# Attention and a routed expert layer on one core: each routed row written to a place of its own, instead of added into running sums

## The chip, the core and the metric

The kernel runs on one core of a Trainium2 chip. The metric is the device time of one execution in microseconds. The five engines (PE multiplies matrices, DVE and ACT work on rows of 128 partitions, POOL issues indirect DMAs and small operations, SP issues DMAs) each run their own list of instructions in order and wait for one another by semaphores; 16 DMA engines move the data.

## The reference, cut to what matters

```
x   = x + attention(layernorm(x), context)         # 32 batches x 100 tokens, width 256; context 361 x 192
h   = layernorm(x)
shared = gelu(h @ ws1 + bs1) @ ws2 + bs2
aff = softmax(h @ Wr + br)                         # 31 experts
routed = sum over the 3 experts e with the largest aff:
             aff[e] * (gelu(h @ We1[e] + Be1[e]) @ We2[e] + Be2[e])
out = x + shared + routed + h
```

There are 3200 tokens, so 9600 routed rows of 256 numbers (1 KB in float32), three for each token.

## The kernel before

**Stages.** The 3200 tokens are 25 tiles of 128. In the attention stage (a loop over steps i = -2 to 36, one batch of 100 tokens each, all engines staggered by a few steps) a tile's residual `resid = x + attention` is made by DVE (L754), normalized to `h` (L855), routed, and three indirect DMAs of POOL (L557) write its rows of `h`, with the experts, the weights and the token's number beside them, into lists per expert in DRAM (`xs`, printed as `expert_rows_in`). SP also stores `resid` (L395) and `h` (L396) of each tile to two DRAM arrays `sums[0]` and `sums[1]`, and once fills a third with zeros (L374).

**The middle.** When all tokens are routed, a table of at most 105 routed tiles (expert, first row) is worked out on DVE (L935 to L968) and PE. Beside it PE runs the shared layer for tiles 0 to 7; DVE copies its result into `tok` (L864).

**The routed loop.** For each of 105 tiles SP loads 128 rows of a list (L455, 6 buffers); PE transposes them (L1260), multiplies by the expert's first matrix (L1271) and the second (L1282, with the matrix in place); ACT copies the transposed rows (L715) and applies gelu (L689). DVE, in `tile`, takes out the token number (L993), finds the weight (L994, L996, L1000), copies the expert's first matrix for the tile after next into one of two buffers (L976, `fetch_w1`), and scales the product (L984, the row `y_sb`). POOL then adds the 128 rows into `sums[t % 3]` by an indirect DMA that accumulates (L579); it waits for the accumulation of three tiles before, since two into the same array at once could lose an addition.

**The closing.** After the last accumulation SP loads the three arrays, in 11 groups of 1 to 3 tiles (L473 to L475), DVE adds them (L1018, L1021) and adds the shared result: from `tok` for tiles 0 to 7 (L1025), and for the 17 late tiles from PSUM, where PE makes it meanwhile (L1177, L1186, L1187; DVE L1031). SP stores the groups to the output (L478). Groups of early and late tiles alternate: (8,11), (0,1), (11,14), (1,3) and so on to (7,8), (23,25).

The order of the work is written out by hand: each engine's list is the order of the calls below.

## Time and profile before

| | us |
|---|---|
| median of 3 runs | 494.28 |
| lowest and highest | 491.18, 496.79 |
| the profiled execution's own time | 494.56 |
| its span, first to last instruction | 492.90 |

The profile is of one execution. "Busy" is time in which an engine executes; `PEld` is PE's loading of weights, which overlaps its products. SPq, POOLq and ACTq are the engines' instruction queues, where a DMA's issue is seen. The granted clock is 1.00 at 2.4 GHz and 0.50 at 1.2 GHz. The stages lie at 0 to 216 us (attention), 216 to 233 us (table and shared layer), 233 to 446 us (routed loop) and 446 to 492.9 us (closing).

### The profile page before, as it was taken

The numbers are of one execution on the slowest core, as the hardware profiler recorded it, in microseconds if no ns is written. First come the engines' busy times: TensorE is split into PE (matmuls) and PEld (weight loads), VectorE is DVE, ScalarE is ACT, GpSimd is POOL, SyncE is SP. The second block draws the span as 40 slices with busy tenths as digits, with TensorE's granted clock in tenths as the row PEclk, the third lists the DMA queues.
The fourth block names the chain that finished last, engine by engine and source line by source line (L and its number), as shares of the span: only waits on it lengthen the run. The fifth ranks groups of instructions, "written<-read, shape, count | busy, mean of one in ns | idle before, by whom it ended". The sixth has DMA issues, their size and how long they took to land.

```text
span 492.9 us, 13620 instructions
## 1 busy us (share of the span) xinstructions
PE 461.0 (94%) x3168; PEld 400.0 (81%) x3168; DVE 357.1 (72%) x1614; ACT 253.7 (51%) x848; POOL 308.7 (63%) x316
## 2 busy tenths in 40 slices
PE   8899979999999998879999999999999999999991
PEld 8677757777777877668999898899999999999891
DVE  4958879999999997773567666666666666661784
ACT  1455747676767667462445454445554555543220
POOL 3312385858585857671588888788888888884000
PEclk9999999999999999989999999999999999999997
DMA  7555668877578944893599999898888888875999
GB/s 241 150 172 151 219 208 255 274 239 257 189 235 286 334 149 154 276 360 105 116 184 187 185 183 181 157 145 138 136 137 137 139 135 138 136 107 101 350 348 322
DMA packets 81151, 97.54 MB, mean 198 GB/s; under 512 B 9201, under 2 KB 65906, under 8 KB 81074
## 3 DMA queue, kind: packets, MB, share of 16 engines
q1 hardware_dynamic: 60786, 70.79, 46.9%
q0 software_dynamic: 19248, 25.40, 30.8%
q10 hardware_dynamic: 1040, 0.48, 0.5%
q8 instruction: 29, 0.48, 0.4%
q14 instruction: 48, 0.39, 0.3%
HBM read 54.91 MB, written 41.73 MB: 196 GB/s over the span
## 4 chain that ended last, share of the span: by engine, by line
PE 50%; DVE 15%; issue 10%; DMA 10%; SPq 5%; POOL 3%; ACT 2%; POOLq 0%; DVEq 0%; ACTq 0%
PE bank L1271 12%; PE bank L1282 12%; DMA sum<-y_sb,token 6%; PE bank L1260 3%; PE bank L1106 2%; PE bank L1107 2%; PE bank L1118 2%; DVE w_all L792 2%; PE bank L1158 2%; DMA xt<-expert_rows_in 2%; POOL sum L579 2%; DVE c L741 2%; DMA w_all<-sum 2%; PE bank L1186 2%; PE bank L1159 2%
## 5 line engine op out<-in xcount | busy, mean ns | idle before, releaser
L579 POOL DMA_INDIRECT sum<-y_sb,token x105 | 170.8, 1626 | 48.0 <-issue 24.1
L689 ACT ACTIVATE up<-bank,b_all 128x128 f32<-128x128 f32 x260 | 81.4, 364 | 102.2 <-PE bank L1271 66.1
L1271 PE MATMUL bank<-xtt,w1b 128*128 128x128 f32 x840 | 111.4, 276 | 0.3 <-ACT xtt L715 0.3
L1282 PE MATMUL bank<-w_all,up 128*128 x420 | 108.8, 382 | 0.1
L1271 PEld LDWEIGHTS bank<-xtt,w1b 128*128 128x128 f32 x840 | 102.1, 192 | 0.8 <-ACT xtt L715 0.5
L984 DVE TENSOR_SCALAR y_sb<-bank,gate,inverse 128x256 f32<-128x256 f32 x105 | 57.1, 544 | 55.4 <-PE bank L1282 54.7
L557 POOL DMA_INDIRECT expert_rows_in<-xt,slot x75 | 74.4, 992 | 24.6 <-issue 24.0
L1282 PEld LDWEIGHTS bank<-w_all,up 128*128 128x128 f32 x420 | 71.7, 191 | 6.1 <-issue 0.2
L976 DVE COPY w1b<-w_all 128x512 f32 x105 | 47.7, 454 | 18.1 <-PE bank L1271 7.5
L715 ACT ACTIVATE xtt<-bank 128x256 f32<-128x256 f32 x105 | 40.2, 384 | 39.3 <-PE bank L1260 38.7
L534 POOL TENSOR_TENSOR rs<-mv,eps_cols 128x5 f32<-128x5 f32 (+1 forms) x32 | 8.0, 252 | 62.2 <-DVE mv L849 62.0
L1260 PE MATMUL bank<-ident,xt 128*128 128x128 f32 x210 | 40.0, 273 | 0.7 <-DMA xt<-expert_rows_in 0.7
L1260 PEld LDWEIGHTS bank<-ident,xt 128*128 128x128 f32 x210 | 29.2, 141 | 11.9 <-DMA xt<-expert_rows_in 1.7
L536 POOL TENSOR_TENSOR rs<-rs,mhalf 128x5 f32<-128x5 f32 (+1 forms) x32 | 36.4, 1137 | 2.5
L1118 PEld LDWEIGHTS bank<-w_all 128*128 128x128 f32 (+1 forms) x192 | 24.1, 191 | 13.1 <-ACT w_all L630 12.5
L792 DVE TENSOR_SCALAR w_all<-w_all,mv,rs 128x192 f32<-128x192 f32 x96 | 31.1, 380 | 2.8 <-POOL rs L536 2.7
L1186 PE MATMUL bank<-w_all,up 128*128 128x256 f32 x100 | 27.3, 397 | 2.0 <-issue 0.8
L1118 PE MATMUL bank<-w_all 128*128 128x100 f32 (+1 forms) x192 | 27.8, 281 | 0.8 <-ACT w_all L630 0.8
L741 DVE BATCH_NORM_STATS2 c<-w_all 128x6 f32<-128x192 f32 x96 | 27.9, 345 | 0.2 <-DMA w_all<-in_ctx 0.2
L1177 PEld LDWEIGHTS bank<-tok,w_all 128*128 128x128 f32 x200 | 26.9, 199 | 1.2
L1177 PE MATMUL bank<-tok,w_all 128*128 128x128 f32 x200 | 27.5, 284 | 0.0
L1106 PE MATMUL bank<-w_all,tok 128*100 128x361 f32 x64 | 25.4, 478 | 0.0
(199 smaller groups left out, 883.4 us busy)
## 6 DMA issues: line engine op xcount, KB each, us to landing
xt<-expert_rows_in SPq DMA_DIRECT2D x105, 132.0 KB, 2.6
w_all<-in_w SPq DMA_DIRECT2D x47, 256.0 KB
w_all<-in_ctx SPq DMA_DIRECT2D x32, 288.0 KB, 3.1
w_all<-sum SPq DMA_DIRECT2D x15, 384.0 KB, 7.3
sum<-pad_rows SPq DMA_DIRECT2D x1, 3328.0 KB, 12.0
w_all<-in_x SPq DMA_DIRECT2D x25, 128.0 KB, 3.1
sum<-y_sb SPq DMA_DIRECT2D x25, 128.0 KB
sum<-xt SPq DMA_DIRECT2D x25, 128.0 KB
```

What stands on the lines that cost most here:

```text
L557: pool.indirect_dma_start(xs, bass.IndirectOffsetOnAxis(ap=slot[s4][:, k:k + 1], axis=0), h_sb[s4][:, :], None).then_inc(scattered[s4], 16)
L579: pool.indirect_dma_start(sums[s], bass.IndirectOffsetOnAxis(ap=token[sx][:, 0:1], axis=0), y_sb[sx][:, :], None, compute_op=ALU.add).then ...
L689: ins = act.activation(up[s][:, m * P:m * P + P], up_ps[s][:, m * P:m * P + P], ACT.Gelu, bias=b1_all[:, e, m:m + 1].rearrange("p o n -> p ...
L715: act.activation(xtt[s][:, :], tile_ps[s], ACT.Copy).then_inc(tile_t_copied, 1)
L792: ins = dve.tensor_scalar(z[s4][:, k, 0:D2], c_sb[s4][:, k, :], mv[s][:, k, 0:1], rs[s][:, 1, k:k + 1], ALU.subtract, ALU.mult)
L976: dve.tensor_copy(w1b[n.slot(2)][:, :], w1_all[:, bass.ds(e, 1), :].rearrange("p o n -> p (o n)"))\
L984: dve.tensor_scalar(y_sb[sx][:, :], down_ps[s], gate[s][:, 0:1], inverse[s][:, 0:1], ALU.mult, ALU.mult).then_inc(y_made, 1)
L1118: mm = pe.matmul(mix_ps, z[s4][0:KT[k], k, 0:P], probs_t[s][0:KT[k], k, :], start=(k == 0), stop=(k == 2))
L1177: mm = pe.matmul(up_ps[s][:, m * P:m * P + P], w1_all[:, NE, c * INTER + m * P:c * INTER + m * P + P], tok[:, c, cut(t)], start=(c == 0), ...
L1260: mm = pe.transpose(tile_ps[s][:, c * P:c * P + P], xt[sx][:, c * P:c * P + P], ident[:, :])
L1271: mm = pe.matmul(up_ps[s][:, m * P:m * P + P], w[:, c * INTER + m * P:c * INTER + m * P + P], xtt[s][:, c * P:c * P + P], start=(c == 0), ...
L1282: mm = pe.matmul(down_ps[s], up[s][:, m * P:m * P + P], w, start=(m == 0), stop=(m == 1))
```

## The change

- Every routed row goes to its own place in one DRAM array `routed_rows`, at row 768 + 3 * token + rank (rank 0, 1 or 2 of its expert for the token). The list rows carry three such places (`DST`) instead of the token's number; the padding rows carry none, and their rows go to one of the 768 spare rows. POOL's indirect DMA is a plain write, and waits for no earlier one; a buffer's earlier write is waited for by DVE, six tiles later.
- DVE's `tile` picks weight and place in one pass (2 x 3 numbers), reduces them before it copies the matrix, and makes the row numbers (`token`) after it.
- `x` is loaded into `base`, one place per tile in SBUF, and `resid` overwrites it there. ACT then turns it into resid + h in place, as base * (1 + rstd) - mean * rstd (`scale_base`): 8 tiles in the attention steps 22 to 29 and 17 in every second tile of the routed loop. For this all steps' mean and rstd are kept (`stats`), in the space of the two matrix buffers. SP's stores of `resid` and `h`, the fill with zeros and the waits for them are gone.
- DVE adds the shared result of tiles 0 to 7 onto `base` at once.
- The closing loads 11 times (3 KB in a row for each token: its three routed rows) instead of 33 times, and DVE adds the three onto `base`, then for late tiles the shared result.
- To make room, one more expert's first matrix is loaded early (24 instead of 23), the late loads are cut differently, and some small arrays move.

```diff
-WHO, EXPS, SUM, TOKEN = D1, D1 + TOP, D1 + 2 * TOP, D1 + 2 * TOP + 1
-ROW = TOKEN + 1
+WHO, EXPS, DST, SUM = D1, D1 + TOP, D1 + 2 * TOP, D1 + 3 * TOP
+ROW = SUM + 1
 SLOTS = 4
+XS = 6
+SPARE = XS * P
...
-    sums = [nc.dram_tensor(f"sum{k}", [TOKENS + P, D1], F32, kind="Internal").ap() for k in range(3)]
+    routed_rows = nc.dram_tensor("routed_rows", [SPARE + TOP * TOKENS, D1], F32, kind="Internal").ap()
...
+        base = sb("base", [P, TILES, D1])
+        shift = sb("shift", [P, 2, 39])
...
-        x_sb = [lend(1, P, D1) for _ in range(8)]
...
+        x_sb = [base[:, t, :] for t in range(TILES)]
...
+        w1b_all = sb("w1b_all", [P, 2, 2 * INTER])
+        fold_q = lend(1, P, 2 * (RQ + NE)).rearrange("p (c n) -> p c n", c=2)
+        first = w1b_all.rearrange("p s n -> p (s n)")
+        stats = first[:, 0:39 * 20].rearrange("p (i k n) -> p i k n", k=5, n=4)
...
+        FIRST_ROWS = 20
+        rows1 = w1_all[:, 0:30, :].rearrange("p e n -> p (e n)").rearrange("p (t k n) -> p t k n", k=TOP, n=D1)
+        rows2 = w2_all[:, 0:9, :].rearrange("p e n -> p (e n)")[:, 0:6 * TOP * D1].rearrange("p (t k n) -> p t k n", k=TOP, n=D1)
...
-                    sp.dma_start(sums[2].rearrange("(k p) n -> p k n", p=P),
-                                 pad_rows[:, 0:D1].unsqueeze(1).to_broadcast([P, TILES + 1, D1])).then_inc(spare_ready, 16)
-                    for k in range(2):
-                        sp.dma_start(sums[k][TOKENS:TOKENS + P, :], pad_rows[:, 0:D1]).then_inc(spare_ready, 16)
...
-                t = ends(i - 5)
-                if t is not None:
-                    sp.wait_ge(h_made, t + 1)
-                    alone(sp)
-                    sp.dma_start(sums[0][cut(t), :], resid[t % SLOTS][:, :]).then_inc(base_out[t % SLOTS], 16)
-                    sp.dma_start(sums[1][cut(t), :], h_sb[t % SLOTS][:, 0:D1]).then_inc(h_out[t % SLOTS], 16)
...
-            sp.wait_ge(resid_made, TILES)
+            sp.wait_ge(gates_made, TILES)
             alone(sp)
-            late1(23, 24)
+            late1(24, 26)
...
-            for s in range(3):
-                sp.wait_ge(added[s], len(range(s, NT, 3)) * 16)
-            def rows_of(dram, lo, hi):
-                return dram[lo * P:hi * P, :].rearrange("(k p) n -> p k n", p=P)
+            for s in range(XS):
+                sp.wait_ge(put[s], len(range(s, NT, XS)) * 16)
             for g, (lo, hi) in enumerate(GROUPS):
-                sp.dma_start(part0[:, lo:hi, :], rows_of(sums[0], lo, hi)).then_inc(rows_in[g], 16)
-                sp.dma_start(part1[:, lo:hi, :], rows_of(sums[1], lo, hi)).then_inc(rows_in[g], 16)
-                sp.dma_start(part2[:, lo:hi, :], rows_of(sums[2], lo, hi)).then_inc(third_in[g], 16)
+                rows = routed_rows[SPARE + TOP * lo * P:SPARE + TOP * hi * P, :]
+                sp.dma_start(rows_at(lo, hi).rearrange("p t k n -> p t (k n)"),
+                             rows.rearrange("(t p k) n -> p t (k n)", p=P, k=TOP)).then_inc(rows_in[g], 16)
             for g, (lo, hi) in enumerate(GROUPS):
-                sp.wait_ge(final_made, final_at[hi - 1])
-                sp.dma_start(rows_of(flat_out, lo, hi), part0[:, lo:hi, :]).then_inc(final_out, 16)
+                if lo < S_E:
+                    sp.wait_ge(sum_made, TOP * g + TOP)
+                else:
+                    sp.wait_ge(shared_added, late_tiles.index(hi - 1) + 1)
+                alone(sp)
+                sp.dma_start(flat_out[lo * P:hi * P, :].rearrange("(t p) n -> p t n", p=P), base[:, lo:hi, :]).then_inc(final_out, 16)
...
+                if i == SHIFT_STEP:
+                    pool.tensor_scalar(shift[:, 0, 0:18], stats[:, 0:18, 4, 3], 1.0, None, ALU.add).then_inc(first_shifts, 1)
+                    pool.tensor_tensor(shift[:, 1, 0:18], stats[:, 0:18, 4, 0], stats[:, 0:18, 4, 3], ALU.mult).then_inc(first_shifts, 1)
+                    pool.wait_ge(first_shifts, 2)
+                    pool.tensor_scalar(shift[:, 1, 0:18], shift[:, 1, 0:18], -1.0, None, ALU.mult).then_inc(first_shifts, 1)
...
+            def put_rows(t):
+                sx = t.slot(XS)
                 pool.wait_ge(token_ready, t.count(1))
                 pool.wait_ge(y_made, t.count(S_E + 1))
-                if t.has(3):
-                    pool.wait_ge(added[s], adds(t, 3))
                 alone(pool)
-                pool.indirect_dma_start(sums[s], bass.IndirectOffsetOnAxis(ap=token[sx][:, 0:1], axis=0),
-                                        y_sb[sx][:, :], None, compute_op=ALU.add).then_inc(added[s], 16)
+                pool.indirect_dma_start(routed_rows, bass.IndirectOffsetOnAxis(ap=token[sx][:, 0:1], axis=0),
+                                        y_sb[sx], None).then_inc(put[sx], 16)
...
+            def scale_base(t):
+                i = LAST[t] + 5
+                act.activation(base[:, t, :], base[:, t, :], ACT.Identity, bias=shift[:, 1, i:i + 1],
+                               scale=shift[:, 0, i:i + 1]).then_inc(base_scaled, 1)
...
+                if SHIFT_STEP + 2 <= i < SHIFT_STEP + 2 + S_E:
+                    t = i - SHIFT_STEP - 2
+                    act.wait_ge(first_shifts, 3)
+                    act.wait_ge(h_made, t + 1)
+                    scale_base(t)
...
+                if t % 2 == 1 and S_E + t // 2 < TILES:
+                    scale_base(S_E + t // 2)
...
-                    if mixed >= SLOTS:
-                        dve.wait_ge(base_out[m4], (mixed // SLOTS) * 16)
-                    dve.scalar_tensor_tensor(resid[m4][:, :], attn_ps[:, 0:D1], rinv[m2][:, 0:1], x_sb[mixed % 8], ALU.mult,
+                    dve.scalar_tensor_tensor(base[:, mixed, :], attn_ps[:, 0:D1], rinv[m2][:, 0:1], x_sb[mixed], ALU.mult,
...
-                dve.tensor_copy(tok[:, :, cut(u)], down_ps[u % 2].rearrange("p (c q) -> p c q", c=2)).then_inc(y_made, 1)
+                dve.wait_ge(base_scaled, u + 1)
+                dve.tensor_tensor(base[:, u, :], base[:, u, :], down_ps[u % 2], ALU.add).then_inc(y_made, 1)
...
+            dve.wait_ge(gates_transposed, 7)
...
-                if t.has(XS):
-                    dve.wait_ge(added[t.slot(3)], adds(t, XS))
-                dve.tensor_copy(token[sx][:, :], xt[sx][:, TOKEN:TOKEN + 1]).then_inc(token_ready, 1)
-                dve.scalar_tensor_tensor(own_exp[s][:, :], xt[sx][:, WHO:WHO + TOP], tile_e[:, t.r:t.r + 1],
-                                         xt[sx][:, EXPS:EXPS + TOP], ALU.is_equal, ALU.mult).then_inc(picked, 1)
+                own_rows = xt[sx][:, EXPS:EXPS + 2 * TOP].rearrange("p (a k) -> p a k", k=TOP)
+                dve.scalar_tensor_tensor(mine[s][:, :, :], xt[sx][:, WHO:WHO + TOP].unsqueeze(1).to_broadcast([P, 2, TOP]),
+                                         tile_e[:, t.r:t.r + 1], own_rows, ALU.is_equal, ALU.mult).then_inc(picked, 1)
                 dve.reciprocal(inverse[s][:, :], xt[sx][:, SUM:SUM + 1]).then_inc(inverse_made, 1)
+                dve.wait_ge(picked, t.count(1))
+                dve.tensor_reduce(gate[s][:, :], mine[s][:, :, :], AX.X, ALU.add).then_inc(gate_made, 1)
                 if more:
                     fetch_w1(t.back(-2))
-                dve.wait_ge(picked, t.count(1))
-                dve.tensor_reduce(gate[s][:, :], own_exp[s][:, :], AX.X, ALU.add).then_inc(gate_made, 1)
+                dve.wait_ge(gate_made, t.count(1))
+                if t.has(XS):
+                    dve.wait_ge(put[sx], t.turn(XS) * 16)
+                dve.tensor_tensor(token[sx][:, :], gate[s][:, 1:2], spare_no[:, sx:sx + 1], ALU.max).then_inc(token_ready, 1)
...
+            dve.tensor_scalar(shift[:, 0, 18:39], stats[:, 18:39, 4, 3], 1.0, None, ALU.add).then_inc(last_shifts, 1)
+            dve.scalar_tensor_tensor(shift[:, 1, 18:39], stats[:, 18:39, 4, 0], -1.0, stats[:, 18:39, 4, 3],
+                                     ALU.mult, ALU.mult).then_inc(last_shifts, 1)
...
+            dve.wait_ge(base_scaled, TILES)
+            def add_late(k):
+                t = late_tiles[k]
+                dve.wait_ge(down_made, S_E + NT + k + 1)
+                dve.tensor_tensor(base[:, t, :], base[:, t, :], last_ps[k % 6], ALU.add).then_inc(shared_added, 1)
             for g, (lo, hi) in enumerate(GROUPS):
-                dve.wait_ge(rows_in[g], 32)
-                dve.tensor_tensor(part0[:, lo:hi, :], part0[:, lo:hi, :], part1[:, lo:hi, :], ALU.add).then_inc(sum_made, 1)
-                dve.wait_ge(sum_made, 2 * g + 1)
-                dve.wait_ge(third_in[g], 16)
-                dve.tensor_tensor(part0[:, lo:hi, :], part0[:, lo:hi, :], part2[:, lo:hi, :], ALU.add).then_inc(sum_made, 1)
-                dve.wait_ge(sum_made, 2 * g + 2)
-                if lo < S_E:
-                    rows = part0[:, lo:hi, :].rearrange("p k (c q) -> p k c q", c=2)
-                    dve.tensor_tensor(rows, rows, tok[:, :, lo * P:hi * P].rearrange("p c (k q) -> p k c q", q=P),
-                                      ALU.add).then_inc(final_made, 1)
-                else:
+                dve.wait_ge(rows_in[g], 16)
+                for k in range(TOP):
+                    if k > 0:
+                        dve.wait_ge(sum_made, TOP * g + k)
+                    dve.tensor_tensor(base[:, lo:hi, :], base[:, lo:hi, :], rows_at(lo, hi)[:, :, k, :], ALU.add).then_inc(sum_made, 1)
+                if lo >= S_E:
+                    dve.wait_ge(sum_made, TOP * g + TOP)
                     for t in range(lo, hi):
-                        k = late_tiles.index(t)
-                        dve.wait_ge(down_made, S_E + NT + k + 1)
-                        dve.tensor_tensor(part0[:, t, :], part0[:, t, :], last_ps[k % 6], ALU.add).then_inc(final_made, 1)
+                        add_late(late_tiles.index(t))
...
-                    pe.wait_ge(final_made, final_at[late_tiles[k - 6]])
+                    pe.wait_ge(shared_added, k - 5)
```

DVE's list for one tile of the routed loop, from one scaled product to the next; `fetch_w1` is the COPY. Before:

```order
L993 CAST token<-xt 128x1
L994 SCALAR_TENSOR_TENSOR own_exp<-xt,tile_e 128x3
L996 RECIPROCAL inverse<-xt 128x1
L321 TENSOR_LOAD table
L321 ISA x2
L976 ISA
L976 COPY w1b<-w_all 128x512
L1000 TENSOR_REDUCE gate<-own_exp 128x1
L984 TENSOR_SCALAR y_sb<-bank,gate,inverse 128x256
```

And now (`mine` takes the place of `own_exp`):

```order
L992 SCALAR_TENSOR_TENSOR mine1<-xt3,gates_all 128x6
L994 RECIPROCAL inverse1<-xt3 128x1
L996 TENSOR_REDUCE gate1<-mine1 128x2
L331 TENSOR_LOAD table
L331 ISA x2
L976 ISA
L976 COPY w1b_all<-w1_all 128x512
L1002 TENSOR_TENSOR token3<-gate1,spare_no 128x1
L984 TENSOR_SCALAR tok<-bank1,gate1,inverse1 128x256
```

The reduction stands ahead of the copy instead of behind it, and the row numbers for POOL, first before, come last but one.

DVE's list in the closing, its first three groups. Before:

```order
L1018 TENSOR_TENSOR w_all<-w_all 128x3x256
L1021 TENSOR_TENSOR w_all<-w_all 128x3x256
L1031 TENSOR_TENSOR w_all<-w_all,bank 128x256 x3
L1018 TENSOR_TENSOR w_all<-w_all 128x256
L1021 TENSOR_TENSOR w_all<-w_all 128x256
L1025 TENSOR_TENSOR w_all<-w_all,tok 128x256
```

And now (`w1_all` holds the loaded rows):

```order
L1035 TENSOR_TENSOR base<-base,w1_all 128x768 x3
L1028 TENSOR_TENSOR base<-base,bank4 128x256
L1028 TENSOR_TENSOR base<-base,bank5 128x256
L1028 TENSOR_TENSOR base<-base,bank6 128x256
L1035 TENSOR_TENSOR base<-base,w1_all 128x256 x3
```

A late group has three adds of loaded rows where it had two; an early group has three where it had three in all.

## Rows read from the trace of the kernel before

**Rows 1.** The page: each engine's busy time (share of the span) x instructions.
```profile
PE 461.0 (94%) x3168; PEld 400.0 (81%) x3168; DVE 357.1 (72%) x1614; ACT 253.7 (51%) x848; POOL 308.7 (63%) x316
```

**Rows 2.** Stretches: us, busy time (x instructions) by engine, clock, DMA share, GB/s.
```profile
128.00:172.00 44.00, 41.58 (x300) 33.23 (x299) 41.84 (x210) 30.39 (x116) 31.01 (x41) 1.00 0.82 264
...
218.00:221.00 3.00, 2.20 (x6) 1.59 (x6) 2.69 (x12) 1.58 (x5) 2.35 (x3) 0.50 1.07 399
...
320.00:340.00 20.00, 20.00 (x142) 18.28 (x140) 12.91 (x61) 10.08 (x30) 16.90 (x11) 1.00 0.90 140
...
464.00:468.00 4.00, 4.00 (x28) 3.74 (x27) 3.82 (x7) 1.25 (x4) 0.00 (x0) 1.00 1.10 348
...
484.00:488.00 4.00, 0.00 (x0) 0.00 (x0) 2.31 (x5) 0.00 (x0) 0.00 (x0) 0.88 1.09 384
```

**Rows 3.** DVE's scaled products and matrix copies: ns min/median/max, first and last start, forms.
```profile
L976 DVE COPY w1b<-w_all x105: 426/427/740, 231.8 to 441.2; 128x512 f32 x105
...
L984 DVE TENSOR_SCALAR y_sb<-bank,gate,inverse x105: 542/544/547, 237.6 to 445.8; 128x256 f32<-128x256 f32 x105
```

**Rows 4.** Timeline, routed loop: start, us, engine, line, operation [idle before <-releaser].
```profile
434.35 0.55 DVE L984 TENSOR_SCALAR y_sb<-bank,gate,inverse 128x256 f32<-128x256 f32 x1 [0.58 <-PE bank L1282]
435.25 0.43 DVE L976 COPY w1b<-w_all 128x512 f32 x1
436.23 0.97 PEld L1271 LDWEIGHTS bank<-xtt,w1b 128*128 128x128 f32 x8
436.32 0.54 DVE L984 TENSOR_SCALAR y_sb<-bank,gate,inverse 128x256 f32<-128x256 f32 x1 [0.58 <-PE bank L1282]
```

**Rows 5.** POOL's accumulating DMAs: durations, first and last start; DMA issues with us to landing.
```profile
L579 POOL DMA_INDIRECT sum<-y_sb,token x105: 1542/1659/1804, 239.0 to 448.9; - x105
...
w_all<-in_x SPq DMA_DIRECT2D x25, 128.0 KB, 3.1
```

**Rows 6.** POOL's plain indirect writes of the attention stage, and their time to landing.
```profile
L557 POOL DMA_INDIRECT expert_rows_in<-xt,slot x75: 956/963/1197, 58.3 to 223.8; - x75
...
DMA to landing us min/median/max: 2.4/3.7/7.5
```

**Rows 7.** The chain that ended last, closing: start, us, what.
```profile
448.92 3.68 DMA sum<-y_sb,token
...
452.68 0.38 SPq L473
...
485.63 0.42 DVE w_all L1031
```

**Rows 8.** Timeline: a shared copy of the middle, then PE and DVE in the closing.
```profile
230.24 0.42 DVE L864 COPY tok<-bank 128x256 f32<-128x256 f32 x1 [2.02 <-PE bank L1187]
...
447.54 1.08 PEld L1177 LDWEIGHTS bank<-tok,w_all 128*128 128x128 f32 x8
449.73 1.08 PEld L1177 LDWEIGHTS bank<-tok,w_all 128*128 128x128 f32 x8
...
457.23 0.96 DVE L1018 TENSOR_TENSOR w_all<-w_all 128x768 f32<-128x768 f32 x1 [10.92 <-DMA w_all<-sum]
...
465.07 1.08 DVE L1031 TENSOR_TENSOR w_all<-w_all,bank 128x256 f32<-128x256 f32 x3
466.07 0.68 DVE L1018 TENSOR_TENSOR w_all<-w_all 128x512 f32<-128x512 f32 x1
466.79 0.69 DVE L1021 TENSOR_TENSOR w_all<-w_all 128x512 f32<-128x512 f32 x1
...
482.23 0.59 PE L1187 MATMUL bank<-b_all,gates_t 128*128 128x256 f32 x2
```

**Rows 9.** DVE's first adds in the closing: ns min/median/max, first and last start, forms.
```profile
L1018 DVE TENSOR_TENSOR w_all<-w_all x11: 415/684/959, 457.2 to 484.2; 128x768 f32<-128x768 f32 x5, 128x512 f32<-128x512 f32 x4, 128x256 f32<-128x256 f32 x2
```

**Rows 10.** The 11 output stores (L478), time from issue to landing.
```profile
DMA to landing us min/median/max: 5.6/6.0/6.6
```

**Rows 11.** ACT's copy of the transposed rows in the routed loop, with its idle time before.
```profile
L715 ACT ACTIVATE xtt<-bank 128x256 f32<-128x256 f32 x40 | 15.4, 384 | 15.3 <-PE bank L1260 15.2
```

More of the change, by code:

```diff
@@ L1005, in _ @@
             dve.wait_ge(expert_in, 16 * EXPERT_DMAS)
[L1006 to L1007 removed]
+            dve.wait_ge(last_shifts, 2)
             for u in range(S_E - 2, S_E):
```

169 lines of the change are left out of this document (74 added, 95 removed).

## The prediction

> **What bounds the kernel now.** I read the stretches first, then each stage's chain. In the attention stage DVE and PE both run at 94 to 95% (the first stretch of [rows 2], 128 to 172 us), the DMA engines at 0.82: the two compute engines hand over to each other, no transfer is waited for. In the routed loop the steady period is the distance of two scaled products, 436.32 - 434.35 = 1.97 us [rows 4], in which PE has no gap; DVE is idle 0.58 us of each. The whole loop took 445.8 - 237.6 = 208.2 us for 104 periods [rows 3]; at 1.97 it would be 104 x 1.975 = 205.4. So 2.8 us of stalls are in it. POOL is the surprise: an accumulating DMA holds it 1.66 us [rows 5], a plain one 0.96 [rows 6]. With waits between, POOL runs as slowly as PE and drags behind: the last product starts at 445.8, the last accumulation at 448.92, and it lands at 452.60 (448.92 + 3.68) [rows 7]. Only then, at 452.68, do the closing loads start.
>
> I count the closing from S, the start of the last scaled product (445.8). Before, loads start at S+6.9, the first sum at S+11.4 (457.23), the last add at S+39.8, the end of the span at S+47.1. It is bound by DMA: 25 tiles x 3 x 131 KB = 9.83 MB in and 3.28 MB out, at 348 and 384 GB/s [rows 2], are 28.2 + 8.5 = 36.7 us; begun at 452.68 plus a fixed 2.3 us (worked out below) this is over at 491.7, 1.2 before the span ends. DVE waits for its groups. PE makes one late tile in 449.73 - 447.54 = 2.19 us and is done at 482.8, S+37.0 [rows 8].
>
> **The change, part by part.**
>
> *Attention.* Gone are 50 stores of 131 KB and a fill of 3.4 MB, all on SP and the DMA engines, neither of which is waited for: nothing. If they slowed something after all, the most to win in the stretch of [rows 2] is DVE's idle time, 44 - 41.84 = 2.2 us. DVE's instructions are the same in number and size. New on ACT are 8 passes over 128x256, by the copy of that size 0.38 us each [rows 11], 3.1 us in all at most if each delays the chain. ACT has 13.6 of 44 us idle there, each pass stands at the end of a step, and PE and DVE are 5% from full; I take +0.3, between -2.2 and +3.1. POOL's three small operations at step 20 lie in its 13 idle us of that stretch. The last weights to be loaded are 0.26 MB more, at 399 GB/s [rows 2] 0.7 us; those loads run at 218 to 221 and the first matrix copy starts at 231.8 [rows 3]: nothing, and with the cover gone 0.7.
>
> *Middle.* The fetch of the table's expert row waits until PE has turned the gates, and DVE gets two short operations: under 1 us of delay, where DVE sat idle 2.02 us before a shared copy [rows 8]. Those copies turn into adds of the same length (0.41 against 0.42). Nothing.
>
> *Routed loop, DVE.* The list has five small operations, a copy and a scaling as before. The reduction, 0.15 us, and its wait now stand ahead of the matrix copy. The copy began at 435.25 and ended at 435.68; PE loads it at 436.23 [rows 4]: 0.55 us of room. I reckon 0.15 to 0.25 us later: nothing. Behind DVE's new wait for a write of six tiles ago (12 us) stand the scaling and, by it, PE's banks; a write lands in 3.7 [rows 6]: nothing.
>
> *Routed loop, ACT.* 17 passes of 0.38, one every second tile, fall into the idle time of 15.3 / 40 = 0.38 before each copy [rows 11]. What spills over delays a copy that PE needs 1.5 us later: nothing.
>
> *Routed loop, POOL and DMA.* An indirect write without accumulation holds POOL 0.96 instead of 1.66 us and moves the bytes one way. Where the stalls came from I cannot read for each, but from 320 us on PE is busy without a gap [rows 2], and before it the padding writes run beside the accumulations. Bounds: none of 2.8 goes, or all. I take 2.4, since the trace has no stall after the paddings end and the load on the queues falls by more than the paddings add. **-2.4.**
>
> *Closing, start.* POOL is no longer behind: the last write is issued when its product is ready, 0.54 us after S, at S+0.6. It lands 2.4 us later at the least, 3.7 in the middle [rows 6]; the accumulation took 3.68 [rows 7]. I take 2.8, near the shortest, since without the reads of the accumulations the DMA engines have less to do at the last tiles. SP issues the loads at S+0.6+2.8+0.1 = S+3.5, against S+6.9.
>
> The Trainium skill (DMA: Bandwidth & Descriptors, section Anatomy of one DMA — SWDGE (gpsimd) path) has a fixed 2.0 us and the bytes at 436 GB/s for such a DMA, 2.3 us for 131 KB; its estimate would put the time 0.5 us below mine, and the shortest landing of 2.4 is close to it.
>
> *Closing, first group.* Before, two loads (0.79 MB) landed in 457.23 - 452.68 = 4.55 us [rows 7, 8]; at 348 GB/s that is 2.26 for the bytes and 2.3 fixed. Now one load of 1.18 MB with rows of 3 KB: 1.18 / 0.399 = 2.95, and 2.3: 5.2 us (bounds 4.55 and, at 348, 5.7). 399 is the rate of the weight loads, whose rows of 2 KB are nearest. DVE starts at S+8.7.
>
> *Closing, DVE.* Start to start, an add of 512 takes 0.72 and three from PSUM take 1.00 [rows 8]; 768 and 256 take 0.96 and 0.415 [rows 9], plus the same 0.04. Five late triples: 3 x 1.0 + 1.0 = 4.0 each, 20.0. Three early pairs: 3 x 0.72, 6.5. Two early single tiles: 3 x 0.455, 2.7. The last pair: 2.16 + 0.75 = 2.9. Sum 32.1 without a gap: S+40.8. A triple arrives in 3.0 to 3.4 us, faster than the 4.0 in which it is used. PE's last tile, S+37, is there too; its wait for a freed bank (0.7 us before) goes.
>
> *Closing, DMA.* S+3.5+2.3 and 24.6 (at 399) + 8.5 gives S+38.9, at 348 S+42.5. So **DVE becomes the bound** and the larger rows are not worth their 3.6 us: after DVE comes one more store. Before, stores took 5.6 to 6.6 us behind a queue [rows 10]; now the queue is empty, and the nearest row is a load of 128 KB in 3.1 us [rows 5]. I take 3.0 (bounds 2.4 and 5.6). End: S+43.8 against S+47.1. **-3.3**; with all bounds together -5.0 to +0.7.
>
> **Sum:** -3.3 - 2.4 + 0.3 = -5.4 us. The profiled execution took 494.56, and 492.9 of it is the span; it gives 489.2. The median of the runs is 0.28 lower: **488.9 us**. All low ends give 484.3, all high ends 498.1.
>
> **Rivals.**
>
> A. *The late POOL was no more than a shadow.* The stalls of the loop come from the loads of list rows and the paddings, which stay, and the last write and last store take as long as before (3.7 and 5.6 us). Closing: -3.3 + 0.9 + 2.6 = +0.2, loop 0, attention +0.3: 494.8; with one of the two 491 to 493. For it: POOL's lag costs the loop nothing by itself, since PE never waits for POOL. Against: stalls end exactly when traffic falls. I put it at 493.
>
> B. *Slower: the matrix copy comes too late.* If reading a 2 x 3 product by a broadcast and waiting for its reduction push the copy back by more than 0.55 us, PE waits in each tile. The point is 0.55; each 0.1 beyond costs 105 x 0.1 = 10.5 us. At 0.7: 15.8 - 5.4, so 504.6. For it: DVE is 72% busy [rows 1], its copy sometimes takes up to 0.74 us [rows 3], and it had four small steps in a queue already. Against: the sum of the small ones moves by one operation of 0.15 us.
>
> C. *ACT's passes are felt.* All 3.1 us in the attention stage: 488.9 + 2.8 = 491.7. For it: ACT feeds both engines at 95%. Against: it is 69% busy there [rows 2].
>
> D. *More comes.* With 10 MB less traffic the attention stage gives up its 2.2 us and all low ends hold: 484.5.
>
> E. *It does not do what it says*, if some other wait holds POOL at the old pace. The lists show the accumulation and its wait gone; 494.
>
> **How the numbers follow.** Forecast 0.50 (its own range 485.5 to 491.5), A 0.27, B 0.09, C 0.07, D 0.05, E 0.02. The range reaches over the forecast, D, C and most of A: 484.5 to 496.5, leaving out B and the ends of A. About 1%, 4.9 us, is what a measurement of this kernel can tell from no change; the border is 489.3, inside the forecast, of which six tenths lie under it: 0.30, with D 0.05 and parts of A and C 0.08 makes faster 0.43. Slower is B and a rest of A, 0.11; within 1% 0.46.
>
> **What would show it.** POOL's indirect writes near 1.0 us, the last within 1 us of the last scaled product. The loop in 205.5 to 206.5 us. First closing loads 3.5 us after S, DVE without a gap for 32 us from S+8.7, the last store alone in about 3 us. Wrong would be: PE waiting for `w1b_all` in each tile (B); gaps in DVE between groups of the closing, so that DMA is the bound still; a first DVE add later than S+10.

## The result, and the profile after

The changed kernel took **502.19 us** (median of 4 runs, 501.05 to 502.71) beside 494.78 us for the kernel before (491.18 to 496.79): ratio 1.018, 95% interval 1.013 to 1.023. Forecast were 488.9 us and a range of 484.5 to 496.5: the sign was wrong and the time lies outside the range. The profiled span is 501.1 us against 492.9. Two executions fell in a slower state of the chip, one of the kernel before (676.68 us) and one of `b3_no_stores` (532.98 us); the medians and ranges below include them, the ratios leave them out.

What was meant to shrink did. DMA traffic fell from 97.5 to 87.5 MB; POOL fell from 308.7 us busy [rows 1] to this (the page's busy times):

```profile
PE 471.8 (94%) x3168; PEld 402.9 (80%) x3168; DVE 365.8 (73%) x1622; ACT 263.1 (53%) x873; POOL 241.2 (48%) x322
```

The span is 8.2 us longer: the routed loop costs 14.8, the stretch up to the first scaled product gives back 2.7 (234.9 for 237.6) and the closing 3.9. These are DVE's matrix copies and scaled products after, to be held against [rows 3]; the last two numbers ahead of the forms are first and last start:

```profile
L976 DVE COPY w1b_all<-w_all x105: 426/427/676, 228.6 to 453.4; 128x512 f32 x105
...
L984 DVE TENSOR_SCALAR tok<-bank,gate,inverse x105: 531/544/547, 234.9 to 457.9; 128x256 f32<-128x256 f32 x105
```

457.9 - 234.9 = 223.0 us, where the kernel before took 208.2 and 104 undisturbed periods would take 205.4. The copy itself is no longer (427 ns). What is new stands ahead of it. DVE's timeline of one tile:

```profile
346.79 0.54 DVE L984 TENSOR_SCALAR tok<-bank,gate,inverse 128x256 f32<-128x256 f32 x1
347.25 0.22 DVE L992 SCALAR_TENSOR_TENSOR mine<-xt,gates_all 128x6 f32<-128x6 f32 x1
347.38 0.16 DVE L994 RECIPROCAL inverse<-xt 128x1 f32<-128x1 f32 x1
347.50 0.16 DVE L996 TENSOR_REDUCE gate<-mine 128x2 f32<-128x6 f32 x1
348.47 0.43 DVE L976 COPY w1b_all<-w_all 128x512 f32 x1 [0.81 <-PE bank L1279]
348.81 0.15 DVE L1002 TENSOR_TENSOR token<-gate,spare_no 128x1 int32<-128x1 f32 x1
348.88 0.54 DVE L984 TENSOR_SCALAR tok<-bank,gate,inverse 128x256 f32<-128x256 f32 x1
```

In [rows 4] the copy follows its scaled product by 0.90 us, here by 1.68, and 0.81 us of that is idle. Over the loop this idle time is 72.9 us in 103 tiles; before it was 7.5 us in 18. The profile names PE's product as its end, but that releaser is a guess among semaphores; the work that fills the gap is in DVE's queue, which counts as no busy time. `fetch_w1` first reads the expert's number from the table into a register (its line is 331 after, 321 before). The queue's three steps of that read in the same tile (duration three times, then start):

```profile
L331 DVEq TENSOR_LOAD <-table x1: 519/519/519, 347.5 to 347.5; - x1
L331 DVEq FUSED_REGOPS  x1: 190/190/190, 348.1 to 348.1; - x1
L331 DVEq SEQ_ASSERT  x1: 23/23/23, 348.3 to 348.3; - x1
```

And in a tile of the kernel before:

```profile
L321 DVEq TENSOR_LOAD <-table x1: 301/301/301, 371.2 to 371.2; - x1
L321 DVEq FUSED_REGOPS  x1: 190/190/190, 371.6 to 371.6; - x1
L321 DVEq SEQ_ASSERT  x1: 23/23/23, 371.8 to 371.8; - x1
```

beside its timeline:

```profile
371.06 0.55 DVE L984 TENSOR_SCALAR y_sb<-bank,gate,inverse 128x256 f32<-128x256 f32 x1 [0.58 <-PE bank L1282]
...
371.72 0.16 DVE L996 RECIPROCAL inverse<-xt 128x1 f32<-128x1 f32 x1
371.97 0.43 DVE L976 COPY w1b<-w_all 128x512 f32 x1
```

Before, the read starts at 371.2 while the scaling (371.06 to 371.61) still executes: the queue had run ahead, and by 371.97 it was done. After, it starts at 347.5, when `mine` ends (347.25 + 0.22): DVE's wait for `picked`, which the reduction needs, now stands ahead of it in the queue. Read, register step and check end at about 348.35, and the copy starts at 348.47. This tile's circle is 0.68 us from the scaling to the end of `mine`, 1.00 to the copy, 0.41 to the next scaling: 2.09 us against PE's 1.975. So DVE's own list has become longer than PE's period. The scaling, which before waited for PE's product in nearly every tile, now mostly follows its list without a wait. The idle time ahead of L984, after:

```profile
  PE bank L1290: 7.5, 21
```

and before:

```profile
  PE bank L1282: 54.7, 100
```

(us, times). PE's products wait by name for the copy in 6 tiles, 1.6 us in all. The mean period is 223.0 / 104 = 2.144; the read takes 387 ns in the median of the loop (519 in the tile shown), where it took 306 before.

The closing went nearly as forecast. The chain of waits, with S, the start of the last scaled product, at 457.88 (start, us, what):

```profile
457.88 0.55 DVE tok L984
459.17 2.42 DMA routed_rows<-tok,token
461.71 5.21 DMA w_all<-routed_rows
467.01 0.97 DVE base L1035
```

Before, in [rows 7, 8], the loads began at S+6.9 and the first add at S+11.4; now at S+3.8 and S+9.1. The stretch below shows DVE without a gap and the DMA engines full (us, busy time (instructions) of PE, PEld, DVE, ACT, POOL, granted clock, DMA share, GB/s):

```profile
470.00:494.00 24.00, 24.00 (x151) 21.99 (x149) 23.31 (x39) 6.60 (x22) 0.00 (x0) 1.00 1.05 397
```

The stores' time from issue to landing, against [rows 10], is now

```profile
DMA to landing us min/median/max: 1.9/6.7/13.8
```

The stores begin at 475.7, while loads are still under way; the last one begins at 498.5 and the span ends 2.6 us later.

The span ends at S+43.2; it ended at S+47.1. POOL is no longer behind; its writes take 0.96 us each, as those of [rows 6] do, and it waits for DVE:

```profile
L567 POOL DMA_INDIRECT routed_rows<-tok,token x105: 959/962/1149, 236.3 to 459.2; - x105
its engine sat idle before it (us, times) until:
  DVE tok L984: 115.4, 88
```

### The profile page after: what moved, and what is told of

Read it like the earlier page. It is cut to its first block, busy times and chain, and to the rows that moved or that the text cites. A ratio compares the mean times of both kernels' runs of the same rounds, so it can differ in the third digit from the quotient of the medians.

```text
span 501.1 us, 13393 instructions
## 1 busy us (share of the span) xinstructions
PE 471.8 (94%) x3168; PEld 402.9 (80%) x3168; DVE 365.8 (73%) x1622; ACT 263.1 (53%) x873; POOL 241.2 (48%) x322
## 3 DMA queue, kind: packets, MB, share of 16 engines
q1 hardware_dynamic: 43170, 60.69, 40.9%
q0 software_dynamic: 9168, 25.49, 13.3%
## 4 chain that ended last, share of the span: by engine, by line
PE 65%; DVE 20%; issue 4%; ACT 3%; DMA 2%; DVEq 1%; ACTq 0%; POOLq 0%; SPq 0%; POOL 0%
PE bank L1279 19%; PE bank L1290 17%; DVE base L1035 5%; PE bank L1268 4%; PE bank L1126 3%; PE bank L1114 3%; PE bank L1115 2%; PE bank L1166 2%; DVE w_all L792 2%; PE bank L1167 2%; PE bank L1194 2%; PE bank L1136 2%; DVE w1b_all L744 1%; PE bank L1154 1%; PE bank L1185 1%
## 5 line engine op out<-in xcount | busy, mean ns | idle before, releaser
L567 POOL DMA_INDIRECT routed_rows<-tok,token x105 | 101.4, 966 | 126.9 <-DVE tok L984 115.4
L1279 PE MATMUL bank<-tok,w1b_all 128*128 128x128 f32 x840 | 116.1, 281 | 2.9 <-DVE w1b_all L976 1.6
L1279 PEld LDWEIGHTS bank<-tok,w1b_all 128*128 128x128 f32 x840 | 101.7, 191 | 11.8 <-issue 7.1
L976 DVE COPY w1b_all<-w_all 128x512 f32 x105 | 45.7, 435 | 73.9 <-PE bank L1279 72.9
L984 DVE TENSOR_SCALAR tok<-bank,gate,inverse 128x256 f32<-128x256 f32 x105 | 57.0, 543 | 10.9 <-PE bank L1290 7.5
L714 ACT ACTIVATE tok<-bank 128x256 f32<-128x256 f32 x105 | 40.2, 384 | 35.6 <-PE bank L1268 35.0
L526 POOL TENSOR_TENSOR w1b_all<-w1b_all,mhalf 128x5 f32<-128x5 f32 (+1 forms) x32 | 36.5, 1140 | 2.5
L792 DVE TENSOR_SCALAR w_all<-w_all,w1b_all 128x192 f32<-128x192 f32 x96 | 31.5, 383 | 0.2 <-POOL w1b_all L526 0.2
L1035 DVE TENSOR_TENSOR base<-base,w_all 128x768 f32<-128x768 f32 (+2 forms) x33 | 24.7, 762 | 9.4 <-DMA w_all<-routed_rows 8.6
L744 DVE BATCH_NORM_STATS2 w1b_all<-w_all 128x6 f32<-128x192 f32 x96 | 27.8, 345 | 0.0
```

The lines of the kernel that those rows point to most:

```text
L567: pool.indirect_dma_start(routed_rows, bass.IndirectOffsetOnAxis(ap=token[sx][:, 0:1], axis=0), y_sb[sx], None).then_inc(put[sx], 16)
L792: ins = dve.tensor_scalar(z[s4][:, k, 0:D2], c_sb[s4][:, k, :], st(i - 1)[:, k, 0:1], st(i - 1)[:, k, 3:4], ALU.subtract, ALU.mult)
L976: dve.tensor_copy(w1b[n.slot(2)][:, :], w1_all[:, bass.ds(e, 1), :].rearrange("p o n -> p (o n)"))\
L984: dve.tensor_scalar(y_sb[sx], down_ps[s], gate[s][:, 0:1], inverse[s][:, 0:1], ALU.mult, ALU.mult).then_inc(y_made, 1)
L1035: dve.tensor_tensor(base[:, lo:hi, :], base[:, lo:hi, :], rows_at(lo, hi)[:, :, k, :], ALU.add).then_inc(sum_made, 1)
L1279: mm = pe.matmul(up_ps[s][:, m * P:m * P + P], w[:, c * INTER + m * P:c * INTER + m * P + P], xtt[s][:, c * P:c * P + P], start=(c == 0), ...
```

## The experiments

Four kernels ran beside the kernel before on one chip (492.05 us there, median of 7 runs), four on a second one on which the kernel before took 513.7 (7 runs), four on a third (492.68, 13 runs). Ratios are against the kernel before on the same chip. "Loop" is the distance from the first to the last scaled product, "stage" from the first to the last `h`, both in the profiled run.

### Undoing only the order

`a1_copy_first`, the changed kernel with `fetch_w1` ahead of the wait:

```diff
+                if more:
+                    fetch_w1(t.back(-2))
                 dve.wait_ge(picked, t.count(1))
                 dve.tensor_reduce(gate[s][:, :], mine[s][:, :, :], AX.X, ALU.add).then_inc(gate_made, 1)
-                if more:
-                    fetch_w1(t.back(-2))
```

> The changed kernel with DVE's matrix copy (and the fetch of its expert number into a register) ahead of the reduction again, as in the kernel before; all else as changed. Theory R (the register fetch, 0.6 to 0.97 us, now starts only after the wait for the picked product and so is no longer hidden behind the scaling): the loop from first to last scaled product falls from 223.0 us to 205.5 to 208, and the time from 502.2 to 485 to 488. Rival W (ACT's passes, the wait for the write of six tiles ago or the wider small operations slow the loop): the loop stays above 218, the time above 497.

Measured: 484.55 us (482.63 to 486.38), ratio 0.986 (0.981 to 0.991). The loop takes 440.0 - 234.7 = 205.3 us, as long as 104 periods without a stall:

```profile
L984 DVE TENSOR_SCALAR tok<-bank,gate,inverse x105: 542/544/546, 234.7 to 440.0; 128x256 f32<-128x256 f32 x105
```

So all of the loss sits in that order. Everything else of the change is worth 1.4%, some 7 us.

`a2_load_early` moves the register read alone; copy and reduction keep the order of the change:

```diff
+                e = table_entry(dve, t.back(-2), 0, NE - 1) if more else None
                 dve.wait_ge(picked, t.count(1))
                 dve.tensor_reduce(gate[s][:, :], mine[s][:, :, :], AX.X, ALU.add).then_inc(gate_made, 1)
                 if more:
-                    fetch_w1(t.back(-2))
+                    copy_w1(t.back(-2), e)
```

> The changed kernel with only the fetch of the expert number into DVE's register moved ahead of the wait for the picked product; the reduction still stands ahead of the copy. Theory R (the register fetch is what is exposed): loop 205.5 to 209 us, time 485 to 489, about as the run with the whole copy first. Rival P (the copy's place behind the reduction is what costs): loop and time stay near 223 and 502.

Measured: 484.56 us (482.19 to 485.63), ratio 0.987 (0.984 to 0.991); loop 436.9 - 231.7 = 205.2. DVE's timeline has the reduction ahead of the copy, without the gap, and idle time only where the product is awaited:

```profile
346.39 0.54 DVE L987 TENSOR_SCALAR tok<-bank,gate,inverse 128x256 f32<-128x256 f32 x1 [0.66 <-PE bank L1294]
...
347.10 0.16 DVE L1000 TENSOR_REDUCE gate<-mine 128x2 f32<-128x6 f32 x1
347.22 0.43 DVE L979 COPY w1b_all<-w_all 128x512 f32 x1
...
348.37 0.54 DVE L987 TENSOR_SCALAR tok<-bank,gate,inverse 128x256 f32<-128x256 f32 x1 [0.66 <-PE bank L1294]
```

Here the copy follows its scaled product by 0.83 us, with the reduction ahead of it; it was 0.90 in [rows 4]. The reduction's place costs nothing, as forecast; the read, with its register step and check, is the whole cost.

### Doing only the order

`b1_reduce_first`, the kernel before with its reduction moved:

```diff
                 dve.reciprocal(inverse[s][:, :], xt[sx][:, SUM:SUM + 1]).then_inc(inverse_made, 1)
+                dve.wait_ge(picked, t.count(1))
+                dve.tensor_reduce(gate[s][:, :], own_exp[s][:, :], AX.X, ALU.add).then_inc(gate_made, 1)
                 if more:
                     fetch_w1(t.back(-2))
-                dve.wait_ge(picked, t.count(1))
-                dve.tensor_reduce(gate[s][:, :], own_exp[s][:, :], AX.X, ALU.add).then_inc(gate_made, 1)
```

> The kernel before with one edit: DVE's reduction of the weight, with its wait, stands ahead of the matrix copy. Theory R: the loop grows from 208.2 us to about 220 (the token's cast goes first here, so the cycle on DVE is the same 2.1 us), the time from 494.8 to 505 to 510. Rival W: the loop stays below 211, the time within 2 us of before.

Measured: 503.57 us (499.80 to 505.96), ratio 1.023 (1.016 to 1.031); loop 457.0 - 237.0 = 220.0, 11.8 more than before. The gap appears with the row sizes and destinations of the kernel before:

```profile
346.59 0.16 DVE L998 TENSOR_REDUCE gate<-own_exp 128x1 f32<-128x3 f32 x1
347.33 0.43 DVE L976 COPY w1b<-w_all 128x512 f32 x1 [0.59 <-PE bank L1271]
```

`a7_fetch_behind`, on the second chip, asks whether it is the wait or the reduction that exposes the read (in the cuts of kernels, `...` marks lines left out):

```diff
                 dve.wait_ge(picked, t.count(1))
+                e = table_entry(dve, t.back(-2), 0, NE - 1) if more else None
                 dve.tensor_reduce(gate[s][:, :], mine[s][:, :, :], AX.X, ALU.add).then_inc(gate_made, 1)
                 if more:
-                    fetch_w1(t.back(-2))
+                    copy_w1(t.back(-2), e)
```

> The changed kernel with one line moved: the read of the expert's number from the table into a register stands right behind DVE's wait for `picked`, ahead of the reduction; the matrix copy stays behind the reduction. Theory R (the register read is exposed whenever a semaphore wait stands right ahead of it, since DVE's queue can no longer do it while earlier instructions execute): the reduction and the copy both wait for it, the loop takes about 220 us, 500 us in all. Rival Q (what costs is only that the read stands behind the reduction itself, whose result it follows): the loop takes 205.3 us as with the read ahead of the wait, 484.6 us.

Measured: 520.37 us (516.10 to 522.48), ratio 1.011 (1.002 to 1.020); loop 474.8 - 250.4 = 224.4 us, beside 206.7 for the two kernels on that chip whose read stands ahead of the wait (`a3_no_h`, `c2_pool_adds`). Now the gap stands ahead of the reduction:

```profile
400.54 0.15 DVE L997 RECIPROCAL inverse<-xt 128x1 f32<-128x1 f32 x1
...
401.31 0.16 DVE L1000 TENSOR_REDUCE gate<-mine 128x2 f32<-128x6 f32 x1 [0.61 <-issue]
401.45 0.43 DVE L979 COPY w1b_all<-w_all 128x512 f32 x1
```

It is the wait ahead of the read. (That chip is slower in the attention stage, 179.6 us for the stage here against 167.4 to 170.5 on the first; so whole times in us are not compared across chips.)

### Where the loop's stalls and the closing's 3.9 us came from

`b2_plain_write`, the kernel before with plain instead of accumulating writes and all its waits; the routed sums are left out, since each write replaces the row:

```diff
-                                        y_sb[sx][:, :], None, compute_op=ALU.add).then_inc(added[s], 16)
+                                        y_sb[sx][:, :], None).then_inc(added[s], 16)
```

> The kernel before with the accumulation taken out of POOL's indirect DMA: a plain write to the same place, with the same waits, so a later row of a token overwrites the earlier one (the sums are left out). If the accumulation made the loop's 2.8 us of stalls and POOL's lag: loop 205.5 to 206.5, last write issued 0.6 us after the last scaled product instead of 3.15, time 489 to 490 (-2.4 loop, -3.4 start of the closing). Rival (the stalls come from list loads and paddings): loop 207.5 to 208.5 and time 491 to 492.

Measured: 486.49 us (485.44 to 486.68), ratio 0.990 (0.987 to 0.993). Loop 439.6 - 233.7 = 205.9 us, 2.3 less than before, although the padding writes are the same: the stalls of [rows 3] came with the accumulations. The closing ends at 483.8, S+44.2, where before it was S+47.1: 2.9 us less. Two parts of it stand in the chain of waits, here with S = 439.60:

```profile
441.02 2.40 DMA sum<-y_sb,token
```

The last write is issued at S+1.4 instead of S+3.1, since POOL is on time, and it lands in 2.40 us instead of 3.68, since it doesn't accumulate. The other 1.0 of the closing's 3.9 us is left for the larger rows, the rows kept in SBUF and the fewer loads; no run takes these apart.

### What bounds the new closing

Three kernels. `a5_two_adds` is `a1_copy_first` without the third routed add, which it leaves out for all tiles:

```diff
                 for k in range(TOP):
+                    if k == TOP - 1:
+                        dve.wait_ge(sum_made, TOP * g + k)
+                        dve.nop(nofuse=True).then_inc(sum_made, 1)
+                        continue
```

> The changed kernel with the matrix copy ahead of the reduction, and one of the three routed adds in the closing left out (so the third rank's rows are missing from the output), with all loads and stores as they are. DVE loses 8.8 of 31.5 us. Theory (DVE is the bound, PE's last tile at S+36.2 next): the span ends at S+39.5 instead of S+43.5, 4 us less. Rival W (DMA right behind): S+41 to S+42.5. Rival (DMA was the bound all along): S+43.5.

Measured: 481.11 us (479.70 to 481.86), ratio 0.979 (0.974 to 0.985), end at 478.0 = S+40.9. In its timeline DVE now waits for loads and for PE:

```profile
461.42 1.95 DVE L1039 TENSOR_TENSOR base<-base,w_all 128x768 f32<-128x768 f32 x2 [0.30 <-DMA w_all<-routed_rows]
...
469.93 0.42 DVE L1028 TENSOR_TENSOR base<-base,bank 128x256 f32<-128x256 f32 x1 [0.67 <-PE bank L1199]
```

The chain that ended last now runs over PE's shared layer up to the last tile, and then over one add:

```profile
472.94 0.45 PE bank L1199 x2
473.38 0.02 issue
473.41 0.42 DVE base L1028
```

The add ends at S+36.7, and the span 4.2 us later; the quickest store takes 3.7 us to land here, 1.9 in the changed kernel. `a1_copy_first`, the kernel it was cut from, ends at S+43.5. So DVE was the bound, and 2.6 of the 8.8 us of adds left out could be had: PE's last tile is the next bound, as the theory had it, but the store behind it takes longer than the changed kernel's last one, so the end lies between the theory's S+39.5 and rival W's S+41. What slows the store isn't shown; from 465 to 475 us the DMA engines are full (share 1.07).

`c3_best`, the changed kernel with the early register read, also puts three shared adds into DVE's idle 8.6 us ahead of the first rows:

```diff
+            for k in range(3):
+                add_late(k)
+            dve.wait_ge(shared_added, 3)
             for g, (lo, hi) in enumerate(GROUPS):
                 dve.wait_ge(rows_in[g], 16)
...
-                if lo >= S_E:
+                if lo >= S_E and g > 0:
```

> The changed kernel with the register read ahead of the wait for `picked`, and DVE's three shared adds of the first late group done before the first rows land, in its idle time. Theory: DVE bounds the closing, which gets shorter by 3 x 0.33 us, S+42.4 instead of S+43.4; ratio to the kernel before about 0.985. Rival: POOL was taken for the adds in c2_pool_adds and slowed DVE; if PE or DMA is the bound instead, the closing stays at S+43.4.

Measured: 484.22 us (483.00 to 487.14), ratio 0.986 (0.980 to 0.993). The span ends at 482.8, S+42.3 (S = 440.5), where 42.4 was expected. `a1_copy_first` ends at S+43.5 and `a2_load_early` at S+43.6. In whole runs that 1 us can't be told; each of the three kernels takes 1.3 to 1.4% less than the kernel before, with intervals that end below 1, where the changed one took 1.8% more.

`c2_pool_adds` has the same, and gives the routed adds of the five early groups to POOL:

```diff
+            pool.wait_ge(y_made, S_E + NT)
+            for j, g in enumerate(range(1, len(GROUPS), 2)):
+                lo, hi = GROUPS[g]
+                pool.wait_ge(rows_in[g], 16)
+                for k in range(TOP):
...
+                    pool.tensor_tensor(base[:, lo:hi, :], base[:, lo:hi, :], rows_at(lo, hi)[:, :, k, :], ALU.add).then_inc(early_sum, 1)
```

> The changed kernel with the register read ahead of the wait for `picked`, and a closing shared out: POOL adds the routed rows of the five early groups (8 tiles), DVE only those of the late ones, and DVE's three shared adds of the first late group stand ahead of the first load. Theory: the closing is bound by DVE (31.5 us without a gap), so with 22 us of adds left PE's last tile at S+36.2 is what ends late; add 0.4 and store 2.5 us give S+39.3 instead of S+43.4, and 484.56 - 4.1 = 480.5 us. Rival W (the DMA engines are the bound right behind DVE: 13.1 MB at 400 GB/s from S+3.8 with 2.3 fixed): S+38.9 at the best, with queues S+41 to S+42.5, 482 to 483.7 us. Rival X (POOL's adds are slow, over 2.5 times DVE's 0.96 us for three tiles, or slow DVE's down beside them): no gain, 484.5 or above.

Measured: 500.51 us (498.59 to 501.08) on the second chip, ratio 0.973 (0.966 to 0.979), but `a3_no_h`, with the closing as changed, has 0.979 on that chip, and the closing ends at 498.5, S+42.7: nothing won over `c3_best`, as rival X had it. Groups of adds (count | busy, mean ns of one | idle before), first two of `c2_pool_adds`:

```profile
L1056 DVE TENSOR_TENSOR base<-base,w_all 128x768 f32<-128x768 f32 x15 | 20.6, 1374 | 4.3 <-DMA w_all<-routed_rows 3.9
L586 POOL TENSOR_TENSOR base<-base,w_all 128x512 f32<-128x512 f32 x9 | 15.5, 1724 | 2.5 <-DMA w_all<-routed_rows 2.0
```

and one of `c3_best`:

```profile
L1042 DVE TENSOR_TENSOR base<-base,w_all 128x768 f32<-128x768 f32 x15 | 14.3, 956 | 2.8 <-DMA w_all<-routed_rows 2.4
```

POOL needs 1.72 us for an add of two tiles (512 numbers in a row), which takes DVE 0.69 in `c3_best`, and DVE's own adds go from 956 to 1374 ns beside it. The Trainium skill (SBUF — State Buffer, section SBUF: two separate sides) says the two engines share a pair of ports that one instruction holds until its end, a DVE operation with two SBUF inputs among them; these rows agree.

### ACT's passes

`a3_no_h` is `a1_copy_first` with `scale_base` replaced by an empty instruction, so that h is missing from the sum:

```diff
-                act.activation(base[:, t, :], base[:, t, :], ACT.Identity, bias=shift[:, 1, i:i + 1],
-                               scale=shift[:, 0, i:i + 1]).then_inc(base_scaled, 1)
+                act.nop(nofuse=True).then_inc(base_scaled, 1)
```

> The changed kernel with the matrix copy ahead of the reduction again, and ACT's 25 passes over `base` left out (so h is missing from the sum). Theory: the 8 passes of 596 ns in the attention stage cost 0.9 us, the 17 in the loop nothing, since the loop has no gap on PE with them: 484.55 - 0.9 = 483.6 us. Rival U (they are hidden altogether): 484.5; rival V (each of the 8 delays the chain by its whole length, 4.8 us): 479.8.

Measured: 502.79 us (502.15 to 505.69) on the second chip, ratio 0.979 (0.972 to 0.986). Loop 457.9 - 251.2 = 206.7 us, the same as with the passes in `c2_pool_adds` (455.8 - 249.1): in the loop they are hidden. The stage is 181.8 us without them, and 179.6 with them in both `a7_fetch_behind` and `c2_pool_adds`: no sign of 0.9 us, and the 2.2 us between them go the other way. Whether the 8 passes of that stage cost some tenths stays open.

### The attention stage's 1.7 us

The prediction had no gain there. The stage takes 213.9 - 46.3 = 167.6 us, before 215.7 - 46.4 = 169.3. The timelines differ at POOL's first indirect write, of before and of after:

```profile
58.29 1.20 POOL L557 DMA_INDIRECT expert_rows_in<-xt,slot  x1 [3.88 <-issue]
```

```profile
54.50 1.19 POOL L552 DMA_INDIRECT expert_rows_in<-xt,slot  x1 [0.18 <-issue]
```

Behind it, in the kernel before, POOL's rstd (one over the standard deviation, for the layernorm) comes late and DVE waits 2.67 us for it, once. `b3_no_stores` asks whether SP's stores do that:

```diff
-                    sp.dma_start(sums[0][cut(t), :], resid[t % SLOTS][:, :]).then_inc(base_out[t % SLOTS], 16)
-                    sp.dma_start(sums[1][cut(t), :], h_sb[t % SLOTS][:, 0:D1]).then_inc(h_out[t % SLOTS], 16)
...
+                    for k in range(3):
+                        sp.dma_start(sums[k].rearrange("(k p) n -> p k n", p=P),
```

> The kernel before without SP's 50 stores of residual and h in the attention stage; in their place the one fill with zeros at step 24 covers all three arrays (so residual and h are missing from the sum), and the waits for the stores are gone. It asks where 1.8 to 2.8 us of the attention stage came from. Theory S (the stores' traffic): POOL's idle time of 3.88 us ahead of its first indirect write is 0.2 us, and the stage from the first to the last h takes 167.5 us instead of 169.3; with the rest as before 492.05 - 1.8 = 490.2 us, and up to 1 more for the fills, which move 6.8 MB at once. Rival T (it is in POOL's own list, where the changed kernel has no wait for x_dev): the 3.9 us stay, the stage takes 169.3, and the time is 491.5 to 493.

Measured: 528.43 us (523.95 to 532.98), ratio 1.031 (1.023 to 1.038). The idle time is still 3.07 us: not the stores. That the kernel is slower than the one before, where 490 to 493 us were expected, has a cause of its own: its three fills, 10 MB one behind the other, held up a load of the context, for which DVE waited once (us, times, longest):

```profile
DVE c L730 <- DMA w_all<-in_ctx: 18.6, 1, 18.6
```

`a8_xdev_wait` and `a9_nop` put back POOL's wait for `x_dev_made`, or an empty instruction in its place, into `a2_load_early`:

```diff
                 if b is not None:
                     pool.wait_ge(ctx_stats, b + 1)
+                    if b >= 2:
+                        pool.nop(nofuse=True)
```

> The changed kernel with the register read ahead of the wait for `picked`, and with POOL's wait for `x_dev_made` from the kernel before put back into each attention step (it is always fulfilled by then). It asks whether POOL's idle time ahead of its first indirect write (3.88, 3.63, 2.46 and 3.07 us in the four runs with the list of before, 0.18 in the six with that of the change) comes with that wait. Theory T (it does): 2.4 to 3.9 us of idle time there, and a stage some 1.8 us longer from first to last h than in c3_best on the same chip. Rival: 0.2 us, and nothing in the stage.

> The same kernel with an empty POOL instruction where a8_xdev_wait has the wait. It tells a wait from a place in the list. Theory I (POOL's instructions are fetched in blocks, and a longer list puts a block's end right ahead of the first indirect write, where an instruction load over queue 14 was seen 2.0 to 2.3 us before the write): idle time of 2.4 to 3.9 us here as in a8_xdev_wait. Theory T (the wait itself): 0.2 us here and the idle time in a8_xdev_wait alone.

Measured: with the wait 485.51 us (484.28 to 487.38), ratio 0.987 (0.981 to 0.992), stage 167.5 us, idle time 0.18. With the empty instruction 487.78 us (486.85 to 489.00), ratio 0.990 (0.987 to 0.993), stage 169.2 us, and POOL's row, of `a9_nop`:

```profile
57.28 1.19 POOL L554 DMA_INDIRECT expert_rows_in<-xt,slot  x1 [2.58 <-issue]
```

The wait is not the cause, and neither theory holds as it stands: T wanted the stall in `a8_xdev_wait` alone, I in both. An instruction that does nothing is enough for a 2.58 us stall, in the one trace taken, and `c3_best` without it has 0.18 and a stage of 167.6. In the five kernels that have the stall an instruction load over queue 14 starts 1.7 to 2.3 us before the write (between 56.0 and 56.5 before, between 55.0 and 55.5 in `a9_nop`); without the stall it starts behind the write (between 55.0 and 55.5 in the changed kernel, write at 54.50), and in `a8_xdev_wait` 3.5 us or more before it. The Trainium skill (Runtime: NRT & Kernel Launch, section Instruction fetch mechanics) has each engine fetch its instructions in blocks, at a cost that is mostly hidden; a fetch that is not hidden is what these rows look like. That it is POOL's own fetch is argued from the times, not shown. Why the wait of `a8_xdev_wait`, with as many instructions, has no stall at that place is open; it has POOL idle 1.9 us longer than `c3_best` at an earlier step (6.46 us before an operation at 35.95, for 4.55).

## Why the prediction was wrong

- **Failed: the step "Routed loop, DVE ... I reckon 0.15 to 0.25 us later: nothing".** It counted the reduction, 0.15 us, as all that costs; it named the wait that moves along and gave it no price. Behind that wait DVE's queue could not run ahead: the register read, register step and check went from cover into the open. In the tile shown the copy follows its scaled product 0.78 us later than before, not 0.15 to 0.25, where DVE had 0.58 us idle per tile and the copy 0.55 us of room. The loop took 223.0 us instead of the 205.8 forecast: +17.2 us, of which other stages give back part (the error of the median is 13.3). The prediction read rows of busy time only; the queue's own rows have 301 + 190 + 23 ns under the scaling, and the order lists `TENSOR_LOAD` behind the reduction.
- **Rival B had the place and nearly the time** (504.6 us; measured 502.19), with the wrong mechanism: not a slow broadcast or a slow reduction, and not PE waiting for `w1b_all` in each tile, which the trace names in 6, but DVE's own list longer than PE's period. That its time comes so near is partly luck: by its formula 0.78 us would cost 105 x 0.23 = 24 us, and the read's exposure costs 17.7 (223.0 against 205.3). It was given 0.09 because the sum of small operations moved by one; the chance belonged to "the copy now stands behind a wait".
- **Right: the loop's stalls (-2.4).** With the read early the loop takes 205.2 to 205.3, -2.9; `b2_plain_write` shows that the accumulations made them.
- **Right in size: the closing (-3.3; measured -3.9).** Its parts missed by some tenths both ways: last write issued at S+1.3, not S+0.6; landed in 2.42, not 2.8; loads S+3.8 for S+3.5; first rows in 5.21 for 5.2; adds 31.5 us for 32.1; tail 2.6 for 3.0. DVE became the bound, as said, and `a5_two_adds` shows it.
- **Right: ACT's loop passes and the middle cost nothing**, though a pass from SBUF to SBUF took 0.60 us, not 0.38. The first scaled product follows the last `h` by 21.0 us, by 21.9 before, and by 19.5 to 22.2 in the kernels of the first and third chips, old and new alike.
- **Missed: attention, +0.3 forecast, -1.7 in the stage.** A stall of 3.88 us was in the trace of before, and it came and went with the make-up of POOL's list; its cause stays open. The +0.3 for ACT's passes was not seen, nor excluded.
- With the one step right, the measured parts give 494.8 - 2.9 - 3.9 - 1.7 = 486.3; `a1_copy_first` and `a2_load_early` ran at 0.986 and 0.987 of the kernel before, 487.8 to 488.4 by that median. The forecast of 488.9 was nearly that of a kernel two lines away.

## What to carry to other kernels

When an instruction moves, list what its engine's queue does for it (register reads above all) and ask what wait now stands ahead of that: here the queue's work was free only while it could run ahead of the engine. Where the order allows it, read registers before the first wait of a loop's body, not where their value is used. And where an idle time is put down to an engine that was done long ago, look in the queue's rows for the work that fills it.

## What the runs showed of the hardware

- A value read from SBUF into a DVE register takes 306 ns in the median of the kernel before and 387 in the changed one (up to 851), and 0.19 us of register steps; exposed, from the wait's end to the copy's start, 1.0 us in the tile shown, the reduction included.
- An accumulating indirect DMA holds POOL 1.66 us and a plain one 0.96, for the same 128 rows, and the last one lands in 3.68 and 2.40 us; in `b2_plain_write` that is worth 1%.
- One empty instruction per step in POOL's list went with one stall of 2.58 us; a fulfilled wait in its place did not.
- Adds on POOL beside DVE's adds of 768 numbers slow these by 44% (1374 for 956 ns).
